# Halved strip transfers, and VectorE's part of the layer norms as steps of their own, in a two-layer transformer kernel

## The reference, cut to what matters

```python
# layer 0: a transformer block, 16 heads of 8 features
xn = ada_ln(x, cond, ln1, aff1)              # layer norm, scaled and shifted from cond
x  = x + mha(xn, xn, xn)                     # self attention, 512 keys
x  = x + mha(x, ctx, ctx)                    # cross attention, 77 keys
xn = ada_ln(x, cond, ln2, aff2)              # site 0 in the kernel
x  = x + gelu(xn @ ffn_w1 + b1) @ ffn_w2 + b2
# layer 1: a routed mixture of three experts
nx = layer_norm(x)                           # site 1 in the kernel
evidence = softmax(nx @ Wq @ (ctx @ Wk).T / sqrt(128)) @ (ctx @ Wv)
combined = [nx, evidence, cond]
probs = softmax(combined @ router_W + router_b)
routed = sum_e probs[e] * (silu(combined @ e_w1[e] + b) @ e_w2[e] + b2)
g = sigmoid(silu(combined @ gate_w1 + b) @ gate_w2 + b)
out = x + g * (routed @ out_w + out_b)
```

## Time and profile before

| | us |
|---|---|
| three timed runs | 279.34, 283.95, 284.93 |
| their median | 283.95 |
| the profiled execution, its own time | 277.5 |
| its span (first to last instruction) | 275.7 |
| PE busy in it | 230.2 (84%) |
| DVE, ACT, POOL busy | 153.1, 157.9, 54.8 |

### The profile page before, as it was taken

How to read it: one execution, slowest core, us unless ns; L and a number is a source line. 1 busy time by engine, 2 the same in 40 slices (tenths; PEclk the granted TensorE clock), 3 DMA queues, 4 the chain that set the end, 5 groups by cost and what they waited for, 6 DMA issues and landing times.

```text
span 275.7 us, 3963 instructions
## 1 busy us (share of the span) xinstructions
PE 230.2 (84%) x1299; PEld 98.8 (36%) x1302; DVE 153.1 (56%) x374; ACT 157.9 (57%) x280; POOL 54.8 (20%) x136
## 2 busy tenths in 40 slices
PE   2978799995898989896898876599779999978982
PEld 1323243431133222221322243232226555553752
DVE  7589587877468867893611457500323461362633
ACT  4353387766368767874898631448622784333730
POOL 5389951023001017211310012200100100100000
PEclk9999999999579999997999999959856999999998
DMA  7964160313010000330000000000000000001001
GB/s 277 394 239 114 52 217 16 102 23 96 0 36 0 4 0 4 115 98 23 2 8 2 0 2 2 2 5 1 0 0 1 2 1 0 0 2 38 0 0 38
DMA packets 6616, 13.20 MB, mean 48 GB/s; under 512 B 1926, under 2 KB 4806, under 8 KB 6182
## 3 DMA queue, kind: packets, MB, share of 16 engines
q1 hardware_dynamic: 5014, 9.03, 9.6%
q0 software_dynamic: 1584, 3.94, 4.6%
HBM read 8.07 MB, written 4.69 MB: 46 GB/s over the span
## 4 chain that ended last, share of the span: by engine, by line
PE 57%; DVE 14%; DMA 10%; ACT 6%; POOL 6%; issue 5%; SPq 2%; DVEq 0%; ACTq 0%; POOLq 0%
PE UP L782 7%; DVE negm L1246 5%; PE ST L756 4%; DMA KS<-scr_k 4%; PE S L730 4%; PE ST L986 3%; PE UP L785 3%; PE ST L981 3%; PE S L937 3%; ACT PT L1068 3%; DMA QX<-scr_q 3%; DMA QS<-mT 2%; PE ST L1005 2%; PE ST L759 2%; PE S L942 2%
## 5 line engine op out<-in xcount | busy, mean ns | idle before, releaser
L1068 ACT ACTIVATE PT<-ST 128x512 f32<-128x512 f32 (+1 forms) x160 | 86.5, 596 | 32.7 <-PE ST L756 24.8
L1246 DVE TENSOR_REDUCE negm<-S 128x1 f32<-128x512 f32 x128 | 79.7, 683 | 25.1 <-PE S L730 25.1
L730 PE MATMUL S<-KS,QS 48*128 48x512 bf16 x128 | 38.5, 392 | 8.9 <-DVE negm L1246 4.6
L756 PE MATMUL ST<-QS,KS 51*128 51x512 bf16 x128 | 39.7, 394 | 1.0 <-DMA QS<-mT 0.7
L782 PE MATMUL UP<-PT,VS 128*32 128x512 f32 x256 | 36.7, 647 | 0.0
L756 PEld LDWEIGHTS ST<-QS,KS 51*128 51x128 bf16 x128 | 10.3, 94 | 35.5 <-issue 30.8
L577 POOL CAST mpart<-negm 128x16 bf16<-128x16 f32 x16 | 3.2, 199 | 95.9 <-DVE negm L1246 55.8
L1250 DVE TENSOR_REDUCE negm<-S 128x4 f32<-128x308 f32 x32 | 13.2, 471 | 9.7 <-PE S L736 9.7
L730 PEld LDWEIGHTS S<-KS,QS 48*128 48x128 bf16 x128 | 9.6, 94 | 24.1 <-issue 17.5
L645 POOL TENSOR_TENSOR rstd<-rstd,half 128x4 f32<-128x4 f32 x4 | 4.1, 1018 | 61.1 <-DVE rstd L1297 61.1
L736 PE MATMUL S<-KX,QX 48*128 48x77 bf16 x128 | 6.8, 197 | 6.8 <-DVE negm L1250 3.4
(11 more groups left out here) (278 smaller groups left out, 353.8 us busy)
## 6 DMA issues: line engine op xcount, KB each, us to landing
w_late<-late SPq DMA_DIRECT2D x1, 3089.5 KB, 11.7
scr_q<-part POOLq DMA_DIRECT2D x2, 384.0 KB, 3.6
QS<-scr_q SPq DMA_DIRECT2D x2, 384.0 KB
KS<-scr_k SPq DMA_DIRECT2D x2, 384.0 KB
QX<-scr_q POOLq DMA_DIRECT2D x2, 384.0 KB, 6.5
xn<-x_nat SPq DMA_DIRECT2D x2, 256.0 KB, 3.7
xT<-x_T SPq DMA_DIRECT2D x1, 512.0 KB, 12.6
scr_q<-part POOLq DMA_DIRECT2D x2, 256.0 KB, 3.4
```

The costliest lines, as they stand in the source:

```text
L730: last = mm(S[:, n % 3, :], QS[r, b, 2 * g + jj, i * P:(i + 1) * P], KS[r, b, 2 * g + jj, :], start=True, stop=True)
L756: mm(ST[:, k % 3, :], KS[r, b, block, kt * P:(kt + 1) * P], QS[r, b, block, :], start=True, stop=True).then_inc(s["st_ready"], 1)
L1068: a(PT[0:rows, n % 2, j, :], ST[0:rows, k % 3, :], ACT.Exp, scale=SCALE).then_inc(s["exp_out"], 1)
L1246: v.tensor_reduce(negm[:, slot, e // 4, e % 2, e // 2 % 2:e // 2 % 2 + 1], S[:, n % 3, :], AX.X, ALU.max, negate=True).then_inc(s["max_out ...
```

## The change

Strips: the transfers of batch 1 and of QX of batch 0 are made in two halves of four blocks. SP issues the first half of the queries and of the keys at round 3 and the second half of both at round 7. Each half has its own semaphore, and the maxima wait for their group's half. POOL issues its four QX transfers in one place.

Norms: DVE's share of `norm` becomes a step `moments` (POOL's power and ACT's copy go with it), and DVE's share of `norm_back` becomes a step `centre`. In the cross stage `moments` stands behind a group of four maxima, and three of the last group's four maxima stand between `centre` and PE's turn. For site 1 of batch 0 both `centre` and the turn stand ahead of the third scores of the last cross round. For site 1 of batch 1, at the end, PE's turn stands behind the third expert.

```diff
-    put(3, 0, ("strips_q1",))
-    put(7, 0, ("strips_k1",))
+    put(3, 0, ("strips1", 0))
+    put(7, 0, ("strips1", 1))
...
-            steps.extend([("mrows", CROSS, 1, 1), ("xblock", 6), ("xblock", 7), ("norm_back", 0, 0)])
-            group_maxima()
+            steps.extend([("moments", 0, 0), ("mrows", CROSS, 1, 1), ("xblock", 6), ("xblock", 7), ("centre", 0, 0)])
+            for _ in range(EVENTS[CROSS] - 1):
+                maxima(len(units))
+            steps.append(("norm_back", 0, 0))
+            maxima(len(units))
...
             put(n + 2, 0, ("norm", 1, 0))
-            put(n + 3, len(ROUND) - 1, ("norm_back", 1, 0))
+            put(n + 2, 0, ("moments", 1, 0))
+            put(n + 3, 4, ("centre", 1, 0))
+            put(n + 3, 4, ("norm_back", 1, 0))
...
-    steps += [("context_value", 0), ("norm", 0, 1)]
+    steps += [("context_value", 0), ("norm", 0, 1), ("moments", 0, 1)]
...
-    steps += [("norm_back", 0, 1), ("router_probs", 0)]
+    steps += [("centre", 0, 1), ("norm_back", 0, 1), ("router_probs", 0)]
...
-    steps += hidden(0, 5, 6) + [("tanh", 0), ("norm", 1, 1)] + hidden(0, 6, 7)
-    steps += [("expert", 0, 1), ("norm_back", 1, 1), ("expert", 0, 2), ("context", 1), ("out", 0)]
+    steps += hidden(0, 5, 6) + [("tanh", 0), ("norm", 1, 1), ("moments", 1, 1)] + hidden(0, 6, 7)
+    steps += [("expert", 0, 1), ("centre", 1, 1), ("expert", 0, 2), ("norm_back", 1, 1), ("context", 1), ("out", 0)]
...
-        def strips(eng, dst, scr, done, k0=0):
+        def strips(eng, dst, scr, done, k0=0, k1=H // 2):
...
-                eng.dma_start(dst[STRIP * q:STRIP * q + STACK, k0:, :].rearrange("p k t -> p (k t)"),
-                              src[:, :, k0:, :].rearrange("i d k t -> i d (k t)")).then_inc(done, 16)
+                eng.dma_start(dst[STRIP * q:STRIP * q + STACK, k0:k1, :].rearrange("p k t -> p (k t)"),
+                              src[:, :, k0:k1, :].rearrange("i d k t -> i d (k t)")).then_inc(done, 16)
...
-                elif step[0] == "strips_q1":
+                elif step[0] == "strips1":
+                    k = step[1] * GROUPS
                     sp.wait_ge(s["stack_q1"], STACK_DMAS)
-                    strips(sp, QS[:, 1, :, :], scr_q[1], s["strips_1"])
-                elif step[0] == "strips_k1":
+                    strips(sp, QS[:, 1, :, :], scr_q[1], s[f"strips_1_{step[1]}"], k, k + GROUPS)
                     sp.wait_ge(s["late_set"], 1)
                     sp.wait_ge(s["stack_k1"], STACK_DMAS)
-                    strips(sp, KS[:, 1, :, :], scr_k[1], s["strips_1"])
+                    strips(sp, KS[:, 1, :, :], scr_k[1], s[f"strips_1_{step[1]}"], k, k + GROUPS)
...
-                    strips(g, QX[:, 0, :, :], scr_q[B], s["strips_qx0"])
+                    for k in (0, GROUPS):
+                        strips(g, QX[:, 0, :, :], scr_q[B], s[f"strips_qx0_{k // GROUPS}"], k, k + GROUPS)
...
-                    pe.wait_ge(s["strips_1"], 2 * STRIP_DMAS)
+                    pe.wait_ge(s[f"strips_1_{g // 2}"], 2 * STRIP_DMAS)
...
-                    pe.wait_ge(s["strips_qx0"], STRIP_DMAS)
+                    pe.wait_ge(s[f"strips_qx0_{g // 2}"], STRIP_DMAS)
```

More of the change, by code:

```diff
@@ L445, in block_program @@
             block_ready block_act block_dve qf_ready qf_out split1
-            stack_q0 stack_k0 strips_0 stack_q1 stack_k1 stack_qx0 stack_kx strips_1 strips_qx0 xblock_ready xblock_act
+            stack_q0 stack_k0 strips_0 stack_q1 stack_k1 stack_qx0 stack_kx strips_1_0 strips_1_1 strips_qx0_0 strips_qx0_1 xblock_ready xblock_act
             ctx_ready ctx_v_ready kxf_out split_x strips_kx vx_out kT1_out v1_out
@@ L640, in _ @@
                     g.tensor_copy(rbias[:, :, :], smalls[:, at:at + B * E].rearrange("p (b e) -> p b e", b=B)).then_inc(s["small_out"], 1)
-                elif step[0] == "norm":
+                elif step[0] == "moments":
                     b = step[2]
@@ L1170, in _ @@
                     nc.scalar.copy(wl("e_w2", at, n), MB[:, 0:n]).then_inc(s["fold_out"], 1)
-                elif kind == "norm" and step[1] == 1:
+                elif kind == "moments" and step[1] == 1:
                     b = step[2]
@@ L1283, in _ @@
                                 ("qx1_out", "rest_qx", "qx2_out", "qx3_out"))
-                elif kind == "norm":
+                elif kind == "moments":
                     site, b = step[1:]
@@ L1297, in _ @@
                     v.tensor_scalar(rstd[:, b * QT:(b + 1) * QT], mv[:, b * QT:(b + 1) * QT, 1], EPS, None, ALU.add).then_inc(s["n_var"], 1)
-                elif kind == "norm_back":
+                elif kind == "centre":
                     site, b = step[1:]
```

## The result

The changed kernel takes 265.43 us, the median of four executions (262.83 to 268.52), where the kernel before took 283.2. The ratio is 0.942, with an interval from 0.923 to 0.960. The profiled execution took 266.03 us with a span of 264.2. The forecast was 268.0. The two halves of it, though, came out differently: the pauses of PE went as worked out, the clock only in part.

What follows compares the result with a forecast made beforehand. PE was taken to bound the kernel, busy 230.2 of 275.7 us, through its idle waits and half clock. Terms 6.4 + 3.0 + 1.1 + 2.4 + 0.8 = 13.7 us off 281.6 gave 267.9, forecast 268; range 262.5 to 276 (8 in 10).

Steps and rivals of the forecast that it cites:

- C: Cross stage: DVE's moments move behind the four reductions of the group before, so `ffn1` begins 1.1 us earlier.
- D: Site 1, batch 0, last cross round: idle before the turn goes, net 0.8 us; shorter half-clock stretch, 1.6; together 2.4.
- E: The end: PE runs the third expert in the idle of 2.24 us; context scores start 0.8 us earlier.
- A: Strips of batch 1: the wait of 3.34 us and some 3 us of half clock behind it go, 6.4 us.
- B: Strips of QX: first halves land before PE asks, so the wait of 2.19 us goes; 3.0 us gained.
- rival 1: Half-clock stretches move and don't go, only the idle is gained: 8.2 us, so 273.4; chance 0.22.
- Rival 2: Shorter pauses in the cross stage also spare the half-clock stretch after C: gain 16.9 us, so 264.7; chance 0.09.
- Rival 3: Strip halves land together, so A and B keep their waits: gain 4.3 us, 277.3; chance 0.05.
- rival 4: SP's strip transfers are paid by the run, not the byte, delaying QS<-mT: +9.3 us, 290.9; chance 0.04.
- What I said would show me wrong: QS<-mT ending a PE wait over 1 us, the QX wait staying, or half clock not falling from 32.3 to about 16.

Runs made afterwards that it cites:

- experiment 1: Kernel before with only SP's strips of batch 1 in halves of four blocks: 277.14 us, beside 282.7 for the kernel before.
- experiment 2: Kernel before with only POOL's strips of QX in halves: 278.43 us, ratio 0.990 (0.974 to 1.006).
- experiment 10: Changed kernel with the old order of the cross stage and of the end put back: 270.47 us, against 268.3 for the changed kernel.
- Experiment 11: Changed kernel with centring and turn of site 1, batch 0 put back behind the third scores' round: 268.13 us.
- experiment 3: Kernel before with both strip edits (batch 1 and QX) and none of the norms: 273.96 us, ratio 0.981.
- experiment 9: Changed kernel with fillers (matmuls, results unused) in PE's pauses: opening 5, cross stage 15, last cross rounds 6; 257.70 us, ratio 0.923 to the kernel before.
- experiment 12: Changed kernel with every strip transfer cut once more, to quarters of 96 KB: 270.30 us, against 268.3 for the changed kernel.
- experiment 8: Changed kernel with six matmuls of unused results in PE's pauses in the last cross rounds only: 261.66 us, beside 268.95 unaltered.

## Why the prediction was right, and where it was not

The measure for C, D and E is the same steps in all fourteen profiles. The length from one PE step to another doesn't depend on what stretches came earlier, so the differences are those of the order alone as long as the clock between the two is the same.

**A, 6.4 forecast, 6.5 measured** (experiment 1). The parts were right too: 3.3 us of idle and 3.2 of clock. The second lot was covered, as said.

**B, 3.0 forecast, 3.2 and 3.3 measured** (experiment 2, and 9.08 - 5.76 in the kernel after). The row of 3.9 us for the landing was 4.6 in the end, and the data moved at a DMA share of up to 0.87, so the four transfers probably shared the engines in part. PE asked 5.5 us after the issue, so a margin was left.

**C, 1.1 forecast, 1.03 measured.** From PE's turn of `xT` to `ffn1` the profiles without C and with full clock take 9.63 us (168.76 to 178.39 before; experiments 1, 2 and 10 the same within 0.01), all with C 8.58 to 8.61. The centring stayed where it was: 5.50 us behind that turn before, 5.54 after. The half-clock stretch behind it stayed, as assumed.

**D, 2.4 forecast, 0.5 measured. This is the step that failed.** From the turn of `xT` (L921 before, L927 after) at site 1 to the same step of batch 1 the profiles with 13.6 or 13.7 us of half clock take 21.17 to 21.21 us without D (before, experiments 1 and 2), and with it 20.56 to 20.73 in five and 20.98 in one: 0.5 us. The idle's 0.8 was a little too much: in the kernel after, 1.42 - 0.21 - 0.68 = 0.53 is what goes. The term of 1.6 for a shorter stretch was wrong altogether. I had inferred from A, where steady work had 9.6 us of half clock behind it, that steady work ends a stretch sooner. Experiment 11 has the idle and 10.2 us, the kernel after has no such idle and 13.7, and experiment 3 has 13 us of half clock with PE at work for 12.72 of them. In the same place a stretch takes one length in one execution and another in the next.

The price of half clock was off as well. I took half of its length. The last rounds take 20.68 us with 13.7 of half clock and 15.79 with none (experiments 9 and 12, 15.80 in 8), which is 0.36 us for each. The cross stage from `ffn1` to the first matmul with the feed-forward's second weights takes 8.42 (186.81 - 178.39 before), 6.3 of it at half clock, and 5.49 with none (experiment 9), 0.46. Over the 80 executions with a known clock a straight line, one height for each kernel, gives 0.30 us of span for a us of half clock, with 0.9 us of scatter. PE shares the path with DVE and ACT, which don't slow down: at either clock a reduction of DVE over 512 columns takes 0.69 us and a cross exponential of ACT 0.59, while eight values matmuls go from 1.07 to 1.93.

**E, 0.8 forecast, 0.75 measured**: from the turn of `xT` to the context scores 8.62 us before and 7.87 in every profile with E.

**The sum, 13.7 forecast.** The steps measured are 6.5 + 3.2 + 1.0 + 0.5 + 0.75 = 12.0, and the two profiles differ by 11.5. The two medians over all executions differ by 14.5 and the means by 15.2. What is over 12.0 I put down to the clock. With half-clock time as twice what the mean clock lacks of 1.00, times the span: at equal half-clock time (the heights of the line) the kernel before stands at 264.9 us and the changed one at 257.0: 7.9 us, about the idle times alone (8.2 by the sum of rival 1). The other 7.3 of the means come from 53.8 us of half clock on average before and 29.2 after, times 0.30. Setting the sum against the middle of the executions and not against the profiled one was right: that one had none of the stretches in the opening and was the quickest of thirty. That 268 met the 268.3 of all eight is partly luck: D was taken for 1.9 us too much, and the kernel before had more half clock on average than the four stretches that the sum was read from.

**Rival 1 (stretches move, they don't go)** was right for D and wrong for A. The Trainium skill ("TensorE: Matmul & The Clock Gate", section "What's actually happening") has the clock watched by a monitor that runs free of the program. What the runs show agrees: the wait for the first strips (3.1 to 3.6 us, three profiles) was followed by 10.2, 10.2 and 3.4 us of half clock and that for QX (2.1 to 2.2 us, three profiles) by 3.4, 3.4 and 6.8, and the first 70 us, where the pauses are the same, hold anything from 0 to 20. But they show more than that rule led me to: across a whole kernel the draw is not the same. A kernel with fewer pauses had less half clock on average: 53.8 us before, 29.2 after, 2.8 with all fillers. **Rival 2** was not seen in the change. It is what the fillers do. **Rivals 3 and 4** are ruled out, 3 by the missing wait, 4 by experiment 12. Rival 3's 277.3 kept both waits, though its own text rules A's out; with B's alone it is 281.6 - 10.7 = 270.9. The Trainium skill ("DMA: Bandwidth & Descriptors", section "Anatomy of one DMA") has a fixed cost of some 2 us for each transfer that GpSimd issues. It doesn't add up here: a lot in 8 transfers takes about as long as in 2 on SP's queue, and POOL's QX in 8 ends no wait of PE.

**What I said would show me wrong:** no wait of PE for QS<-mT was over 0.58 us, and no wait for strips is left. The half clock, read in windows of 1 us, fell from some 34 us (32.3 by the coarser reading of the forecast) to 20.5 and not to 16, by the length of D's stretch; so this last sign came in part.

**Open:** the strips or the norms alone already had less half clock on average (41 to 46 us) than the kernel before, though the profile with the norms alone has a stretch in the place of each of the four. Four executions each don't settle whether that is chance. Why the opening's stretch comes in some executions wasn't found either; ahead of it stand pauses of 0.49, 0.23 and 1.43 us in executions with and without it. Nor was a kernel tried with the opening's and the last rounds' fillers but without those of the cross stage.

## What to carry to other kernels

A wait of 2 to 3 us in a stream that keeps PE busy costs one and a half times to twice its length here, because the clock falls behind it (3.3 us cost 6.5, and 2.2 cost 3.2). So first look at which transfer ends such a wait, and cut the part that is asked for first out of it; two more transfers in a queue with slack cost nothing. Then look at the pauses of 0.4 to 1.5 us that are left: no reordering got the clock back, and 26 matmuls into a free bank, some 0.25 us each, were worth 10.6 us (268.3 to 257.7) and made the time repeatable. And before a difference of a few per cent is explained, compare the granted clocks of several executions, and the same step of the timeline in several profiles, which tells 0.5 us where medians of four don't tell 3.

## What the runs showed that I had not expected

- One program on one core had granted clocks between 0.860 and 0.934 in 26 executions (277.5 to 290.1 us). The lengths of half clock in a profile were near 3.4, 6.8, 10.2 or 13.7 us in nearly every case.
- Pauses far shorter than the strip waits go with half clock. In the cross stage, with PE's pauses of 0.4 to 1.3 us (2.1 where C's order is the old one), it came in all twelve profiles without fillers there and in neither of the two with them; in the last rounds (pauses of 0.4 to 0.7 us ahead of it) in eleven of the twelve without and in neither with.
- The fillers cost nothing in the two later stages: from the turn of `xT` to `ffn1` are 8.58 us with twelve of them between and 8.60 without, and the last rounds at full clock take 15.79 us with and without (experiments 9 and 12).
